# A two-layer kernel of scan, attention and expert layers: GpSimd's weight split cut into pieces between scatters, shared-unit work moved to the end, and one decay moved in the first scan

## The reference

```python
x = x + ssm_scan(ctx, layernorm(x))             # selective scan, 16 states
x = x + experts32_top8(layernorm(x))            # every expert computed, masked weights
x = x + cross_attention(layernorm(x), ctx)      # 16 heads, 8 kv heads
x = x + ffn1(layernorm(x))                      # shared + 16 experts, top 2
# ffn1:
shared = _swiglu(x, wg_s, wu_s, wd_s) * 0.1
for e in range(16):
    routed = routed + mask[..., e:e+1] * _swiglu(x, wg[e], wu[e], wd[e])
return shared + routed
```

## Time and profile before

| | |
|---|---|
| median of 3 executions | 668.95 us (668.75 to 670.51) |
| the profiled execution's own time | 668.65 us |
| its span, first to last instruction | 666.9 us |
| mean granted TensorE clock | 0.98 |
| busy: PE, DVE, ACT, POOL | 612.8, 480.9, 411.7, 307.2 us |

### The profile page before, as it was taken

One profiled execution on the slowest core, in us unless ns is written; L12 is line 12 of the kernel. 1 busy time (PEld: TensorE's weight loads), 2 busy tenths in 40 slices (PEclk: granted clock), 3 DMA queues, 4 the chain that ended last, 5 costly groups with the idle time before them and its releaser, 6 DMA issues.

```text
span 666.9 us, 11178 instructions
## 1 busy us (share of the span) xinstructions
PE 612.8 (92%) x3736; PEld 512.5 (77%) x3736; DVE 480.9 (72%) x1046; ACT 411.7 (62%) x845; POOL 307.2 (46%) x306
## 2 busy tenths in 40 slices
PE   6656779999999999999999999999999999969995
PEld 2355544666777888888888999999999988759984
DVE  5999999999975665446557666667678865754455
ACT  4886666775336546445567777877867677624441
POOL 1456630122344334445456655765546788240314
PEclk9689989999999999999999999999999999989999
DMA  6677865667563263544339422242111212344644
GB/s 201 184 254 271 292 215 165 194 204 221 161 191 118 93 199 124 157 157 135 105 99 351 152 80 81 83 151 84 32 32 46 75 67 70 120 132 150 210 151 126
DMA packets 58151, 98.90 MB, mean 148 GB/s; under 512 B 7016, under 2 KB 26992, under 8 KB 58096
## 3 DMA queue, kind: packets, MB, share of 16 engines
q1 hardware_dynamic: 56560, 94.00, 44.4%
q0 software_dynamic: 1536, 4.20, 2.0%
HBM read 78.51 MB, written 19.66 MB: 147 GB/s over the span
## 4 chain that ended last, share of the span: by engine, by line
PE 65%; DVE 16%; issue 7%; ACT 7%; POOL 2%; DMA 1%; another core or an unknown queue 1%; DVEq 0%; SPq 0%; POOLq 0%; ACTq 0%
PE bank L101 18%; PE bank L103 17%; PE bank L102 17%; DVE state L1571 6%; PE bank L911 3%; PE bank L999 2%; ACT bank L1112 2%; POOL w_lo L2202 1%; PE bank L963 1%; DVE u_sb L1496 1%; PE bank L692 1%; PE bank L579 1%; ACT probs L1368 1%; DVE x_tok L1610 1%
## 5 line engine op out<-in xcount | busy, mean ns | idle before, releaser
L2202 POOL TENSOR_TENSOR w_lo<-w_raw,w_hi 128x512 fp32r<-128x512 f32 (+1 forms) x78 | 120.6, 1548 | 153.8 <-ACT w_hi L1076 80.4
L101 PE MATMUL bank<-xt_hi,w_hi 128*128 128x512 f32 x256 | 104.4, 408 | 1.6 <-POOL w_lo L2202 1.0
L103 PE MATMUL bank<-xt_hi,w_lo 128*128 128x512 f32 x256 | 101.1, 395 | 0.0
L102 PE MATMUL bank<-xt_lo,w_hi 128*128 128x512 f32 x256 | 100.8, 394 | 0.0
L1076 ACT ACTIVATE w_hi<-w_raw 128x512 fp32r<-128x512 f32 (+1 forms) x78 | 56.6, 726 | 47.6 <-PE bank L103 45.5
L1368 ACT ACTIVATE probs<-scores,row_min 128x256 f32<-128x256 f32 x128 | 63.8, 501 | 15.8 <-DVE row_min L2009 15.8
L2315 POOL TENSOR_TENSOR probs<-probs,row_scale 128x512 f32<-128x512 f32 x64 | 66.6, 1041 | 5.0
L2009 DVE CUSTOM_DVE_ANT_0 scores<-bank,mask_bias 128x256 f32<-128x256 f32 x128 | 48.8, 420 | 17.3 <-PE bank L103 17.3
L1076 ACT ACTIVATE probs_t_hi<-bank 128x512 fp32r<-128x512 f32 x64 | 38.2, 598 | 32.7 <-PE bank L911 32.3
L101 PEld LDWEIGHTS bank<-xt_hi,w_hi 128*128 128x128 f32 x256 | 48.2, 188 | 12.3 <-POOL w_lo L2202 3.6
L103 PEld LDWEIGHTS bank<-xt_hi,w_lo 128*128 128x128 f32 x256 | 48.1, 188 | 11.7
(11 more groups left out here) (263 smaller groups left out, 1820.2 us busy)
## 6 DMA issues: line engine op xcount, KB each, us to landing
w_raw<-in_ffn_w SPq DMA_DIRECT2D x46, 384.0 KB, 3.5
b_rows<-bc_scratch SPq DMA_DIRECT2D x32, 256.0 KB, 5.0
c_rows<-bc_scratch SPq DMA_DIRECT2D x32, 256.0 KB, 4.0
w_raw<-fold_scratch SPq DMA_DIRECT2D x32, 256.0 KB, 2.8
experts<-in_ffn_w SPq DMA_DIRECT2D x16, 384.0 KB, 4.3
route_bc<-route_scratch SPq DMA_DIRECT2D x31, 192.0 KB, 3.4
slots_scratch<-nothing SPq DMA_DIRECT2D x2, 2944.0 KB, 13.3
slots_in<-slots_scratch SPq DMA_DIRECT2D x22, 256.0 KB, 2.8
```

The lines of the kernel that those rows point to most:

```text
L101: e.matmul(out, w_hi, m_hi, start=first, stop=False)
L102: e.matmul(out, w_hi, m_lo, start=False, stop=False)
L103: return e.matmul(out, w_lo, m_hi, start=False, stop=last)
L2202: e.tensor_tensor(lo[:, 0:n], w_raw[(p - WHOLE) % RAW][:, 0:n], hi[:, 0:n].bitcast(F32), ALU.subtract).then_inc(sem("w_lo"), 1)
```

## The change

Five edits. (1) In the first scan, `scan_decay(0, 2)` on ACT moves from behind `normalise_z(0)` to between the two columns of `activate_delta(1)`, and `normalise_z(1)` from behind it to behind `scan_decay(0, 3)`. (2) Of unit U0 only gate stays in round 6; up moves to round 25, into the place where the gate of U0 + 1 was, and down behind all of U0 + 1. The PSUM banks of the shared units change with it. (3) At the seam of the halves, `turn_slots(12)` moves from the start of round 11 to its end, and `turn_hid(11)` and `down_slots(10)` from the end of round 12 to its start; ACT's and DVE's parts move alike. (4) On POOL the low part of the last weight piece, one instruction of 768 columns ahead of the scatters, becomes three of 256 columns, behind the second, fourth and sixth scatter. (5) At the end, DVE adds most routed rows of half 1 ahead of the shared sum, `add_routed` no longer waits for `added(9, ...)` but `add_acc(9, ...)` for `routed`, and the last output store is one of two chunks where it was two of one chunk.

```diff
-        FILLED = {PAIRS - 6: (U0, ("gate",)), PAIRS - 5: (U0, ("up",))}
+        FILLED = PAIRS - 6
...
-                return ((3, 3), (4, 5), (3, 7), (4, 5))[u - U0]
+                return ((3, 5), (4, 3), (7, 5), (4, 3))[u - U0]
...
             for r in range(1, ROUNDS + 2):
-                if r > 1:
+                if r == PAIRS:
+                    turn_hid(r - 1)
+                    down_slots(r - 2)
+                if r > 1 and r != PAIRS - 1:
                     find_experts(r + 1)
                     turn_slots(r + 1)
...
-                turn_hid(r - 1)
-                if r == ROUNDS + 1:
-                    gate_up(U0 + 1, ("gate",))
-                down_slots(r - 2)
+                if r != PAIRS:
+                    turn_hid(r - 1)
+                    if r == ROUNDS + 1:
+                        gate_up(U0, ("up",))
+                    down_slots(r - 2)
+                if r == PAIRS - 1:
+                    find_experts(r + 1)
+                    turn_slots(r + 1)
...
-                if r in FILLED:
-                    u, sides = FILLED[r]
-                    gate_up(u, sides)
-                if r == PAIRS - 3:
-                    down(U0)
-            gate_up(U0 + 1, ("up",))
+                if r == FILLED:
+                    gate_up(U0, ("gate",))
+            gate_up(U0 + 1)
+            down(U0)
             gate_up(U0 + 2)
             down(U0 + 1)
             gate_up(LAST)
...
-            activate_delta(1)
+            activate_delta(1, (0,))
+            scan_decay(0, 2)
+            activate_delta(1, (1,))
             make_skip(0)
             normalise_z(0)
             for n in range(DS):
-                if n + 2 < DS:
+                if 0 < n < DS - 2:
                     scan_decay(0, n + 2)
-                if n == 0:
+                if n == 1:
                     normalise_z(1)
...
-                    at.wait_ge("routed", TOP1 * HC + 2 * pair + 2)
+                    at.wait_ge("routed", TOP1 * HC + HC + 2 * pair + 2)
...
                         at.wait_ge(*last_back(j))
-                        at.wait_ge(*added(9, j // 2))
...
+            for u in range(U0, LAST):
+                multiply_hidden(u)
+                rest_hidden(u)
             add_acc(8, 0)
             add_acc(8, 1)
+            add_routed(1, range(HC // 2))
             multiply_hidden(LAST)
-            add_routed(1, range(HC))
+            add_routed(1, range(HC // 2, TOP1 * HC - 1))
             add_acc(9, 0)
+            add_routed(1, (TOP1 * HC - 1,))
             add_acc(9, 1)
-            add_routed(1, range(HC, TOP1 * HC))
...
+            def rest_third(p, k):
+
+                cut = slice(k * WIDTH, (k + 1) * WIDTH)
+                hi, lo = w_split[split_slot[p]]
+                at.wait_ge("w_hi", nth_split(p))
+                last = e.tensor_tensor(lo[:, cut], w_raw[(p - WHOLE) % RAW][:, cut], hi[:, cut].bitcast(F32), ALU.subtract)
+                if k == 2:
+                    last.then_inc(sem("w_lo"), 1)
...
             rest_weights(FFN1_PIECES)
-            rest_weights(FFN1_PIECES + 1)
             for i in range(TOP1 * HC):
                 scatter_x(1, i)
+                if i % 2 == 1 and i < 6:
+                    rest_third(FFN1_PIECES + 1, i // 2)
```

More of the change, by code:

```diff
@@ L1090, in move_x_dbl, with activate_delta @@
                 copy(x_dbl[:, h * HT:(h + 1) * HT], bank[6][0:DR + 2 * DS, :], "x_dbl_sb")
-            def activate_delta(h):
-                for c in range(EH):
+            def activate_delta(h, columns=range(EH)):
+                for c in columns:
                     at.wait_ge("dt", 2 * h + c + 1)
@@ L1449, in _ @@
             for r in range(1, ROUNDS + 2):
+                if r == PAIRS:
+                    keep_slots(r - 2)
                 if r > 1:
+                    if r != PAIRS - 1:
+                        copy_slots(r + 1)
+                    activate_slots(r)
+                if r not in (3, 4, PAIRS):
+                    keep_slots(r - 2)
+                if r == PAIRS - 1:
                     copy_slots(r + 1)
-                    activate_slots(r)
-                if r != 4 and r != 3:
-                    keep_slots(r - 2)
                 if r <= SHARED_CHUNKS:
@@ L1466, in _ @@
                     e.preload_act_table_set("silu_and_others")
-                if r in FILLED:
-                    u, sides = FILLED[r]
-                    if "gate" in sides:
-                        activate_gate(u)
-                    if "up" in sides:
-                        round_hidden(u)
+                if r == FILLED:
+                    activate_gate(U0)
+            round_hidden(U0)
             for u in range(U0 + 1, U0 + U1):
@@ L2153, in _ @@
                     transition(7, 12)
-                if r > 1:
+                if r == PAIRS:
+                    copy_hid(r - 1)
+                if r > 1 and r != PAIRS - 1:
                     rest_slots(r + 1)
@@ L2157, in _ @@
                     multiply_slots(r)
+                if r not in (1, PAIRS):
                     copy_hid(r - 1)
+                if r == PAIRS - 1:
+                    rest_slots(r + 1)
                 if r == 2:
@@ L2167, in _ @@
                     find_weights(7)
-                if r in FILLED and "up" in FILLED[r][1]:
-                    multiply_hidden(FILLED[r][0])
-                    rest_hidden(FILLED[r][0])
                 if PAIRS + 7 <= r <= PAIRS + 10:
                     add_routed(0, range(2 * (r - PAIRS - 7), 2 * (r - PAIRS - 6)))
-            multiply_hidden(U0 + 1)
-            rest_hidden(U0 + 1)
-            multiply_hidden(U0 + 2)
-            rest_hidden(U0 + 2)
+            for u in range(U0, LAST):
+                multiply_hidden(u)
+                rest_hidden(u)
             add_acc(8, 0)
             add_acc(8, 1)
+            add_routed(1, range(HC // 2))
             multiply_hidden(LAST)
-            add_routed(1, range(HC))
+            add_routed(1, range(HC // 2, TOP1 * HC - 1))
             add_acc(9, 0)
+            add_routed(1, (TOP1 * HC - 1,))
             add_acc(9, 1)
-            add_routed(1, range(HC, TOP1 * HC))
         @block.gpsimd
@@ L2422, in load_routes, with store_out @@
                     loaded[0] += 1
-            def store_out(k, pair, parts=range(2)):
-                t = half_of(k) * HC + 2 * pair + parts[0]
+            def store_out(k, pair):
+                t = half_of(k) * HC + 2 * pair
                 at.wait_ge("added", 2 * (k - 4) + pair + 1)
-                at.wait_ge("routed", (k - 8) * TOP1 * HC + HC + 2 * pair + parts[-1] + 1)
-                n = len(parts)
-                e.dma_start(out_dram[:, t:t + n, :], x_tok[:, t:t + n, :]).then_inc(sem("out_stored"), 16)
+                e.dma_start(out_dram[:, t:t + 2, :], x_tok[:, t:t + 2, :]).then_inc(sem("out_stored"), 16)
             load(in_proj_sb[:, :], in_proj_t, "ld_in_proj")
@@ L2543, in _ @@
                 store_out(8, pair)
-            store_out(9, 0)
-            for part in range(2):
-                store_out(9, 1, (part,))
+            for pair in range(HC // 2):
+                store_out(9, pair)
             at.wait_ge("bc_stored", 16 * HALVES)
@@ L2550, in _ @@
             at.wait_ge("route_stored", 16 * HALVES)
-            at.wait_ge("out_stored", 16 * (CHUNKS // 2 + 1))
+            at.wait_ge("out_stored", 16 * CHUNKS // 2)
 def kernel(**inputs):
```

## The result

| | before | after |
|---|---|---|
| median (6 executions each) | 668.85 us (668.39 to 670.51) | 662.89 us (661.59 to 664.43) |
| ratio, 95% interval | | 0.9904 (0.9888 to 0.9920) |
| profiled execution, its span | 668.65, 666.9 us | 661.59, 659.8 us |
| granted clock | 0.98 | 0.987 |

Of the 7.1 us that the span is shorter, the page of the kernel after shows 2.6 as busy time of PE (610.2 for 612.8, with the same 3736 matmuls) and 4.5 as idle time of PE. The busy part is the clock: behind the hole before, PE ran at a granted clock of 0.62 to 0.70, and one turn of four matmuls took 1.09 us instead of 0.60.

A forecast was written before the change was run, and what follows sets the result against it. PE, busy 92%, was taken as the bound, with idle time from completions held during dense indirect DMAs. -0.5 (first scan) - 7.5 (middle) + 1.1 (tail) = -6.9: 661.75 us against 668.65, or 662.1 as median; range 659.3 to 669.5.

The forecast's parts named there:

- the hole: PE's idle stretch around half 1's scatters: busy only 0.79 of 5 us at 595 to 600, clock 0.62 and 0.70.
- the hold: At dense scatters and gathers: PE's completions reach other engines late, released 1.6 to 2.1 us after the last DMA ends.
- held all the same: Rival at the scatters: completions stay held until 2.1 us after the last scatter despite the thirds; 667.0 us, chance 0.25.
- First scan, -0.5: DVE's third scan: earlier decay removes at most its 0.71 us idle; 0.5 us gain taken.
- The bound of 0.8: First scan: upper limit of the gain, whose bounds were 0 and 0.8 us.
- Scatters, +2.25: POOL, half 1's scatters: three thirds at 0.75 us each make the last scatter start 2.25 us later, at 595.7.
- Middle, -7.5: Scatters to slots 14: turn 12 6.9 us earlier, 1.4 less behind it, 0.8 lost to the clock.
- The shorter way from turn 12 to 14: PE, rounds 11 to 12: work already done shortens this stretch from 5.44 to 4.0 us, 1.4 less.
- The cold clock of 0.8: Middle: PE's waits of 2.1 and 1.5 us drop its clock, costing 0.8 us, between 0 and 1.5.
- Tail, +1.1: End of program: 2.8 us more PE work, completions held until 661.2, end at 668.0, a loss of 1.1 us.
- so the gathers start when they did: Tail: up of U0 replaces the gate of U0 + 1 before the last down_slots, leaving the gathers' start unchanged.
- The slower one: Rival: completions held at scatters and, one unit earlier, in the tail (+3.1 us); 671.5 us, chance 0.15.

The follow-up runs named there:

- third group: Two runs where the kernel before takes 668.88 us: weight-piece thirds alone added to before, 662.00 us (0.9889); changed kernel without the thirds, 667.77 us (0.9981).
- before_again: The kernel before, unchanged, run again in a later group with the changed kernel: 669.58 us in its one run.
- b_scan: Kernel before with only the first-scan reordering on ACT added: 658.89 us against 659.68 for before there, ratio 0.9983.
- a_whole_2: Changed kernel with the last weight piece's low part again one 768-column instruction ahead of the scatters: 667.77 us against 668.88 for before there, ratio 0.9981.
- a_seam_old: Changed kernel with the reordering at the seam of the halves undone, slots 12 turned at round 11's start: 663.17 us, ratio 0.9903 to before there.
- a_whole: Changed kernel with the last weight piece's low part again one instruction ahead of the scatters: 660.85 us against 659.68 for before there, ratio 1.0014.
- a_unit_old: Changed kernel with U0's move undone (up in round 7, down in round 9 again): 661.56 us against 670.15 for before there, ratio 0.9883.
- b_thirds_2: Kernel before with only the weight piece's thirds put between the scatters: 662.00 us against 668.88 for before there, ratio 0.9889.
- a_gather_gap: Changed kernel plus three POOL subtractions between the last eight gathers, run twice: 662.34 us (1.0036 to before at 659.68) and 663.20 us (1.0047 to 659.74).
- b_thirds: Kernel before with only the weight piece's thirds put between the scatters: 659.72 us against 659.68 for before there, ratio 1.0001.

## Why the prediction was right, step by step

**What bounds, and the hold.** That eight scatters without a break make the hole, and that the thirds between them remove it, is shown by the third group, in both directions. What delays the completions, and whether it is the delivery of PE's signals as I read it, no run shows. What the reading lacked is that the hold depends on the chip or on something that lasts through a group of runs (each group had one chip and one time, so these two aren't told apart): it was there in three sets of runs and absent in two. Its end was read wrong too. I had completions let go 1.6 to 2.1 us after the last indirect DMA; the 3.96 us wait of the earlier trace rows ended at 593.16, before the last scatter had even started (593.42), and in after the wait of 1.71 us ended at 652.28, before the last gather was over (652.67). So the completions come late, by amounts that differ from wait to wait; they are not kept until the issuing ends. The rival "held all the same" is refuted where it could be tested. A wait of 6.4 us for a product of PE (before_again) is more than the Trainium skill has in TensorE: Matmul & The Clock Gate, "The cost: per-tile semaphore tail", which knows completions serialised at some 26 ns and none held for microseconds; in the two sets without the hold no run here contradicts it.

**First scan, -0.5.** Right in kind, somewhat small. The profile that I read had the shortest of five waits (0.71; the mean is 1.54). The bound of 0.8 came from one execution, and the wait depends on when PE's product comes. It measured 0.64 in the first comparison's traces, 0.8 by medians in b_scan, and 1.7 by the mean starts of the first scatter, of which 0.6 stay once the chance in the choice of executions is taken off.

**Scatters, +2.25.** The thirds took 0.85, 0.75 and 0.75 us (0.74 by the slope of the earlier trace rows), and the last scatter starts 11.05 us behind the first for 8.98: +2.07.

**Middle, -7.5.** Measured -7.73, from terms that partly cancel. Turn 12 comes 16.51 us behind the first scatter where it came 23.65: -7.14, beside -6.9. The shorter way from turn 12 to 14 was to give 1.4 and gave 0.59: it took 4.85 us (5.44 before) instead of 4.0, since slots 13 came 1.06 late, while the DMA engines were full (share 1.00, 321 GB/s, windows above). By edits, the thirds alone give 7.05 (29.09 to 22.04), and all edits of the order together the remaining 0.7 (22.04 to 21.36). The cold clock of 0.8 did not come: the clock stays 1.00 through 580 to 610, with waits of 0.43 and 1.06 us at the turns where I had put 2.1 and 1.5. In the holes it did fall: to 0.66 in a_whole_2, whose longest idle time of PE was 2.44 us, and to 0.63 in before_again. There the trace agrees with the Trainium skill, TensorE: Matmul & The Clock Gate, "What's actually happening", by which a PE that idles falls to half clock; behind the waits of up to 1.06 us in after, and behind the 2.38 us of a_seam_old, the rows show 1.00. That the 0.8 was not due here rests on the waits being short; the size of the term was not tested.

**Tail, +1.1.** Measured +1.27: right in size by luck, for a wrong reason. I said that completions held until the gathers end make the loss, and that prompt ones would make a gain of 1.0. But after's order takes 54.64, 54.64 and 54.73 us in the tail on chips that hold, and 54.53 (a_whole) on one that doesn't; before's takes 53.3 with the hold and 51.1 without. So where nothing is held, after's order loses 3.4 in the tail, and the hold hides 2.2 of it by making before slow. a_unit_old, which has edit (5) without edit (2), had 52.24 with a "remote" wait of only 0.4 us: by that, an estimate across chips, edit (2) costs 2.4 and edit (5) 1.1. The rows of DVE in a_whole's tail say why:

```profile
652.41 1.28 DVE L2072 SCALAR_TENSOR_TENSOR x_tok<-back,weight_of,x_tok 128x256 f32<-128x256 f32 x3 [1.95 <-DMA back<-outs_scratch,slot_of_token]
653.61 0.68 DVE L1619 TENSOR_TENSOR x_tok<-x_tok,bank 128x512 f32<-128x512 f32 x1
654.32 0.48 DVE L2072 SCALAR_TENSOR_TENSOR x_tok<-back,weight_of,x_tok 128x256 f32<-128x256 f32 x1
654.91 0.69 DVE L1619 TENSOR_TENSOR x_tok<-x_tok,bank 128x512 f32<-128x512 f32 x1
```

and in b_scan's, which has before's order:

```profile
652.94 1.67 DVE L2066 SCALAR_TENSOR_TENSOR x_tok<-back,weight_of,x_tok 128x256 f32<-128x256 f32 x4 [0.54 <-DMA back<-outs_scratch,slot_of_token]
```

In both, DVE's last work waits for a gather, not for PE. It starts 48.74 us behind turn 14 in a_whole and 46.84 in b_scan, 1.9 later, and has 3.2 us to do instead of 1.67: the two adds of the shared sum now stand behind the gather that they needn't wait for. In after the same stretch of DVE starts 48.91 us behind turn 14 (654.07), so the 1.71 us wait for a product of PE moved the end by 0.2 us at most. The step that failed is "so the gathers start when they did". They start 37.79 us behind turn 14 in after, 36.19 in b_thirds_2 and 36.07 in a_unit_old, so edit (2) delays them by 1.7 (in all fourteen traces: 37.4 to 37.8 with edit (2), 36.0 to 36.2 without). The last `down_slots` stands where it did (33.4 and 33.3 behind turn 14), but the last two stores of slots land later, though they are issued at the same distance: the final one takes 2.8 us in after and 1.7 in b_thirds_2, the 256 KB one before it 4.1 and 2.6. In that stretch both traces have one DMA of instructions (0.02 MB); that it stands in the stores' way in after is a guess, no run tried it, and the cause of the late stores stays open.

**The rivals.** None decided. The slower one did not come in after (one wait of 1.7 to 1.9 us in the tail). But the chance for something like it was real: where there is a hold, the dense gathers went with longest waits of 0 us (a_whole_2), 0.4 (a_unit_old), 2.0 (before), 2.9 (b_thirds_2) and 3.5, twice and beginning with the SiLU of unit LAST, in a_seam_old, whose tail was 1.4 us longer for it or for the order.

**The whole.** Where completions are not held, the changed kernel itself wasn't run. Its pieces there are 21.4 (a_gather_gap, equal to it up to the gathers) and 54.5, beside 21.7 and 51.1: 3.1 lost, less the 0.8 that the medians give the first scan, an estimate of 2.3 us slower than before. a_gather_gap's two medians, less the price of its later gathers, give 1.5 and 2.6. There the thirds themselves cost 1.4 us in after's order (a middle of 21.37 for 19.99 in a_whole), and nothing in before's. The version that the pieces point to is edits (1) and (4) alone. Without the hold (4) alone costs nothing (1.0001) and (1) gives 0.17%; with it (4) gives as much as all five. The two together were not run.

## What to carry to other kernels

A wait whose releaser the profile can't name ("remote") beside an engine that issues indirect DMAs back to back is worth a try with ordinary work moved between them: the work cost nothing here in before's order (1.0001) where nothing was held, and the gaps gave 1.1% where something was. Test a cause and its cure on the same chip, and look at what the kernel before does there first: the same two programs (before and b_thirds) differ by 1.1% on one chip and not at all on another. One profile gives one sample of a wait; where it depends on a product whose time varies, read it in several executions before bounding it, and see where those executions stand beside the median.

## What the runs showed of the hardware

The unchanged kernel takes 659.7 us in two sets of runs, on two chips, and 668.9 to 670.2 us in three others; no chip is on record in two sets, so the chip and the time of the run aren't told apart. The difference lies in the stretches of dense indirect DMAs. Where the hold occurs, a break of 0.75 us of POOL work behind each second DMA (0.9 to 1.0 us from the end of one to the start of the next, for 0.30) is enough for the hole to go; the longest wait of PE left among the scatters of after is 0.93 us, at 589.17. The late starts come both in the middle of the dense indirect DMAs (593.16 in before, 592.98 in before_again) and up to 2.1 us after them (596.45). And before the scatters of half 1 begin, executions of one kernel already differ by over 1 us (584.44 and 585.79 for before, 1.6 of it there at the third scan, 33.11 and 34.71, through the start of one product of PE; 583.68 and 584.73 for a_whole and a_whole_2, where the third scan doesn't wait and the cause wasn't looked for).
